# Two of four k chunks turned by DMA in fp16 parts, and the order of every engine laid out anew, in a batched attention and feed-forward kernel

## The reference

```
q = softmax(Wq LN(x), over the 64 rows of each of 8 heads) / 8      # 512 x 1024
k = softmax(Wk ctx, over the 1024 columns); v = Wv ctx              # 512 x 1024
a = Wo (per head: (v k^T) q) + bo
x = x + a / max(|a| of each column, 1e-12) * g * sqrt(128)
x = x + (LN(x) @ W4 + bias)     # W4: 1024 x 1024, 4-bit numbers with a scale and a zero for each output
```

## Time and profile before

| | us |
|---|---|
| median of 3 runs | 670.4 |
| lowest and highest | 669.9, 672.28 |
| the profiled execution, its own time | 670.46 |
| its span in the trace | 668.7 |
| PE busy, share of the span | 633.6, 95% |
| DVE busy | 550.3, 82% |
| POOL busy | 468.5, 70% |
| ACT busy | 455.1, 68% |

### The profile page before, as it was taken

One profiled execution on the slowest core, in us unless ns is written; L12 is line 12 of the kernel. 1 busy time (PEld: TensorE's weight loads), 2 busy tenths in 40 slices (PEclk: granted clock), 3 DMA queues, 4 the chain that ended last, 5 costly groups with the idle time before them and its releaser, 6 DMA issues.

```text
span 668.7 us, 10173 instructions
## 1 busy us (share of the span) xinstructions
PE 633.6 (95%) x3285; PEld 385.1 (58%) x3302; DVE 550.3 (82%) x897; ACT 455.1 (68%) x741; POOL 468.5 (70%) x409
## 2 busy tenths in 40 slices
PE   3869699999999999999999999999999999999987
PEld 2536365565656656565665656656665656566443
DVE  5786898888888888798888889888888988888854
ACT  3566868577775858777585867768586876858532
POOL 4166575977869596886959687795959778695930
PEclk9959899999999999999999999999999999999999
DMA  8153424756354565735355574635547453524551
GB/s 304 43 121 79 93 57 94 190 96 153 84 132 116 93 181 96 189 63 154 84 96 172 96 190 72 157 80 108 153 95 190 94 144 87 117 65 94 111 143 63
DMA packets 179236, 79.35 MB, mean 119 GB/s; under 512 B 168536, under 2 KB 170096, under 8 KB 179184
## 3 DMA queue, kind: packets, MB, share of 16 engines
q1 hardware_dynamic: 172848, 55.64, 40.2%
q10 hardware_dynamic: 6336, 23.07, 10.2%
HBM read 28.85 MB, written 8.39 MB: 56 GB/s over the span
## 4 chain that ended last, share of the span: by engine, by line
PE 83%; DVE 6%; ACT 3%; POOL 3%; issue 2%; DMA 1%; another core or an unknown queue 0%; SPq 0%; POOLq 0%; DVEq 0%; ACTq 0%
PE ps_m L1224 14%; PE ps_m L1319 14%; PE ps_k L1154 5%; PE ps_ta L1208 4%; PE ps_k L1155 4%; PE ps_k L1156 4%; PE ps_q L1154 4%; PE ps_q L1156 4%; PE ps_q L1155 4%; PE ps_tb L1208 4%; PE ps_o L1156 4%; PE ps_o L1154 4%; PE ps_o L1155 4%; PE ps_o L1419 4%; PE ps_o L1237 2%
## 5 line engine op out<-in xcount | busy, mean ns | idle before, releaser
L457 POOL TENSOR_TENSOR q_tok_lo<-q_exp,q_tok_hi 128x1024 f16<-128x1024 f32 x64 | 137.7, 2153 | 90.0 <-ACT q_tok_hi L611 88.4
L430 POOL TENSOR_TENSOR q_exp<-q_exp,q_rec 128x1024 f32<-128x1024 f32 x64 | 121.7, 1902 | 5.0
L586 ACT ACTIVATE k_exp<-ps_k,k_nmax 128x1024 f32<-128x1024 f32 x64 | 71.0, 1109 | 76.7 <-DVE k_nmax L858 76.7
L1224 PE MATMUL ps_m<-k_t,c_t 128*128 128x512 f32 x256 | 119.1, 599 | 0.0
L600 ACT ACTIVATE q_exp<-q_exp,w_unit 128x512 f32<-128x512 f32 x128 | 92.0, 720 | 39.0 <-DVE q_exp L870 39.0
L865 DVE TENSOR_REDUCE q_nmax<-ps_q 128x8 f32<-128x512 f32 x128 | 87.7, 685 | 27.6 <-PE ps_q L1156 27.2
L858 DVE TENSOR_REDUCE k_nmax<-ps_k 128x1 f32<-128x1024 f32 x64 | 77.3, 1208 | 19.7 <-PE ps_k L1156 19.7
L870 DVE TENSOR_TENSOR q_exp<-ps_q,q_nmax 128x512 f32<-128x512 f32 x128 | 88.5, 692 | 4.4
L611 ACT ACTIVATE q_tok_hi<-q_exp 128x1024 f16<-128x1024 f32 x64 | 67.5, 1055 | 23.6 <-POOL q_exp L430 23.6
L877 DVE TENSOR_REDUCE q_sum<-q_exp 128x16 f32<-128x1024 f32 x64 | 77.3, 1209 | 0.9 <-ACT q_exp L600 0.8
L1154 PE MATMUL ps_k<-c_hi,wk_lo 128*128 128x512 f32 x128 | 67.5, 527 | 3.3 <-ACT k_exp L586 3.2
(11 more groups left out here) (191 smaller groups left out, 1292.5 us busy)
## 6 DMA issues: line engine op xcount, KB each, us to landing
x_res<-in_x ACTq DMA_DIRECT2D x16, 512.0 KB, 3.8
out_x<-y SPq DMA_DIRECT2D x15, 512.0 KB, 2.9
x_in<-in_x ACTq DMA_DIRECT2D x14, 512.0 KB, 5.5
c_in<-in_ctx ACTq DMA_DIRECT2D x14, 512.0 KB, 6.2
x_in<-in_x SPq DMA_DIRECT2D x2, 512.0 KB, 5.8
c_in<-in_ctx SPq DMA_DIRECT2D x2, 512.0 KB, 7.7
q_hi<-q_tok_hi SPq DMA_TRANSPOSE x64, 3.1
q_lo<-q_tok_lo SPq DMA_TRANSPOSE x64, 3.2
```

The source lines that it names most:

```text
L430: nc.gpsimd.tensor_tensor(pair, pair, rec.unsqueeze(2).to_broadcast([P, 2 * HEADS, DH]), ALU.mult).then_inc(qs_done, 1)
L457: nc.gpsimd.tensor_tensor(q_tok_lo[p % 2][:], q_exp[:, 2 * p:2 * p + 2, :].rearrange("p t d -> p (t d)"), q_tok_hi[p % 2][:], ALU.subtract ...
L1224: last = nc.tensor.matmul(ps_m[:], c_t[s][:, t, :], k_t[:, t, :], start=(t == 0), stop=(t == TC - 1))
```

## The change

Chunks 0 and 1 of k are no longer turned on PE. Both are projected for the next batch at a period's end. Their exponentials are lifted by a factor 2^12 (`k_bias`), cut into an fp16 part on ACT (`high_k`) and the rest on POOL (`low_k`), and turned by four DMA transposes on SP's queue (`turn_k`). The turned context is scaled by `c_fit` and kept in f32, in fp16 and as an fp16 rest (`move_tc` has two operations for each half, `low_tc` is new on DVE, with `fit_c` and `undo_g` in place of `fit_g`). `mix_m` makes, for each t, three fp16 matmuls of 256 columns for chunks 0 and 1 and one f32 matmul of 256 columns for chunks 2 and 3. `split_rs` goes from ACT to POOL. `sum_q` of pair 3 goes from the end of its period to the next one, behind `low_x2`, and the order of all engines is laid out anew; `reciprocal` of k's sums goes to mid-period. In the set-up, splits and projections of the first batch come before the preparation of rows, which moves to period 0; the 4-bit weights are unpacked in other places, two at a time, with x2n_hi and x2n_lo lying in `spare`. The core of the diff (PE's, ACT's and DVE's order for periods after 0; indented less than in the file):

```diff
+k_lift = sb("k_lift", [P, 1])
+k_bias = sb("k_bias", [P, TURNED])
+k_hi = [sb(f"k_hi{j}", [P, N], F16) for j in range(TURNED)]
+k_lo = [sb(f"k_lo{j}", [P, N], F16) for j in range(TURNED)]
+k_t_hi = sb("k_t_hi", [P, TC, TURNED * P], F16)
+k_t_lo = sb("k_t_lo", [P, TC, TURNED * P], F16)
+k_t = sb("k_t", [P, TC, HID - TURNED * P])
...
+    def turn_k(b, j, name):
+        tok, turned, done, turned_sem = ((k_hi, k_t_hi, khi_done, khi_turned) if name == "hi" else
+                                         (k_lo, k_t_lo, klo_done, klo_turned))
+        sp.wait_ge(done, TURNED * b + j + 1)
+        if b > 0:
+            sp.wait_ge(m_ready, b)
+        sp.dma_start_transpose(turned[:, :, j * P:(j + 1) * P], tok[j][:]).then_inc(turned_sem, 16)
...
         if do_c:
             turn_q(c, 2, "hi")
+            turn_q(c, 2, "lo")
+        if do_a:
+            turn_k(a, 0, "hi")
...
         if do_f:
...
-            sp.dma_start_transpose(x2_hi[:], x2n_hi[:]).then_inc(x2hi_turned, 16)
+            sp.dma_start_transpose(x2_hi, x2n_hi).then_inc(x2hi_turned, 16)
+            sp.wait_ge(x2lo_done, f + 1)
+            sp.dma_start_transpose(x2_lo, x2n_lo).then_inc(x2lo_turned, 16)
+        if do_a:
+            turn_k(a, 0, "lo")
+            turn_k(a, 1, "hi")
         if do_c:
-            turn_q(c, 2, "lo")
             turn_q(c, 3, "hi")
-        if do_f:
-            sp.wait_ge(x2lo_done, f + 1)
-            sp.dma_start_transpose(x2_lo[:], x2n_lo[:]).then_inc(x2lo_turned, 16)
+        if do_a:
+            turn_k(a, 1, "lo")
         if do_c:
             turn_q(c, 3, "lo")
         if do_a:
...
+        def low_k(b, j):
+            pool.wait_ge(khi_done, TURNED * b + j + 1)
+            if begun(b):
+                pool.wait_ge(klo_turned, 16 * TURNED * b)
+            nc.gpsimd.tensor_tensor(k_lo[j][:], k_exp[:, j, :], k_hi[j][:], ALU.subtract).then_inc(klo_done, 1)
...
+        def split_rs():
+            pool.wait_ge(x2n_done, f + 1)
...
+        if do_f:
+            fit_x2(f)
+        low_k(a, 0)
+        if do_f:
+            split_rs()
+        if do_c:
+            scale_q(c, 3)
+        low_k(a, 1)
+        if do_c:
+            low_q(c, 3)
         if i == 0:
...
         def exp_k(b, sums, j):
             act.wait_ge(kmax_done, 4 * b + j + 1)
-            if begun(8 * b + 2 * (j - 2) + 2):
-                act.wait_ge(tk_ready, 8 * b + 2 * (j - 2) + 2)
-            nc.scalar.activation(k_exp[:, j % 2, :], ps_k[:], ACT.Exp, bias=k_nmax[:, j:j + 1],
+            bias = k_nmax[:, j:j + 1]
+            if j < TURNED:
+                if begun(b):
+                    act.wait_ge(kexp_done, 4 * (b - 1) + j + 1)
+                nc.scalar.activation(k_bias[:, j:j + 1], bias, ACT.Identity,
+                                     bias=k_lift[:]).then_inc(kbias_done, 1)
+                act.wait_ge(kbias_done, TURNED * b + j + 1)
+                bias = k_bias[:, j:j + 1]
+            held, of = (j - 2, b) if j >= 2 else (j + 2, b - 1)
+            if of >= 0:
+                if held < TURNED:
+                    act.wait_ge(klo_done, TURNED * of + held + 1)
+                else:
+                    act.wait_ge(tk_ready, TK * of + 2 * (held - TURNED) + 2)
+            nc.scalar.activation(k_exp[:, j % 2, :], ps_k[:], ACT.Exp, bias=bias,
                                  accum_out=k_sum[:, sums, j:j + 1]).then_inc(kexp_done, 1)
 
-        first = i == FIRST
+        def high_k(b, j):
+            act.wait_ge(kexp_done, 4 * b + j + 1)
+            if begun(b):
+                act.wait_ge(khi_turned, 16 * TURNED * b)
+                act.wait_ge(klo_done, TURNED * (b - 1) + j + 1)
+            nc.scalar.activation(k_hi[j][:], k_exp[:, j, :], ACT.Copy).then_inc(khi_done, 1)
...
         def move_tc(h):
 
+            turned = (ps_ta, ps_tb)[h][:].rearrange("p (t c) -> p t c", t=4)
             act.wait_ge(tc_ready, 2 * n + h + 1)
+            act.wait_ge(cfit_steps, 2 * (n + 1))
             if h == 0 and begun(n - 1):
                 act.wait_ge(m_ready, n - 1)
-            nc.scalar.activation(c_t[1 - s][:, 4 * h:4 * h + 4, :],
-                                 (ps_ta, ps_tb)[h][:].rearrange("p (t c) -> p t c", t=4),
-                                 ACT.Copy).then_inc(tc_moved, 1)
+            nc.scalar.activation(c_t_hi[1 - s][:, 4 * h:4 * h + 4, :], turned, ACT.Identity,
+                                 scale=c_fit[:]).then_inc(cthi_done, 1)
+            nc.scalar.activation(c_t[1 - s][:, 4 * h:4 * h + 4, :], turned, ACT.Identity,
+                                 scale=c_fit[:]).then_inc(tc_moved, 1)
...
+        else:
+            move_m()
+            if do_f:
                 normalise_x2()
...
+            exp_q(0)
+            if do_f:
                 high_x2()
...
+            exp_k(a, s, 2)
+            high_k(a, 1)
+            if do_n:
+                high_c()
+            exp_q(1)
+            high_q(c, 3)
+            move_tk(0)
+            move_tk(1)
+            if do_f:
+                move_rs()
...
+            exp_q(2)
+            exp_k(a, s, 3)
+            squares(0)
+            exp_q(3)
+            high_q(a, 0)
+        move_tk(2)
+        move_tk(3)
+        exp_q(4)
...
+        exp_q(5)
+        if do_c:
+            squares(1)
+        load_ahead()
+        high_q(a, 1)
+        exp_q(6)
+        if do_n:
+            move_tc(0)
+            high_x()
+            exp_k(n, 1 - s, 0)
+            high_k(n, 0)
+        exp_q(7)
+        if do_n:
+            move_tc(1)
+        high_q(a, 2)
+        if do_n:
+            exp_k(n, 1 - s, 1)
...
+        def fit_c():
+            dve.wait_ge(ctop_done, n + 1)
+            if begun(n):
+                dve.wait_ge(fit_steps, 2 * n)
+                dve.wait_ge(ctlo_done, 2 * n)
+                dve.wait_ge(tc_moved, 2 * n)
+            nc.vector.tensor_scalar(c_unit[:], c_top[:], UNIT_FLOOR, 1.0 / C_RANGE, ALU.max,
+                                    ALU.mult).then_inc(cfit_steps, 1)
+            dve.wait_ge(cfit_steps, 2 * n + 1)
+            nc.vector.reciprocal(c_fit[:], c_unit[:]).then_inc(cfit_steps, 1)
+        def low_tc(b, sb_, h):
+            dve.wait_ge(tc_moved, 2 * b + h + 1)
+            nc.vector.scalar_tensor_tensor(out=c_t_lo[sb_][:, 4 * h:4 * h + 4, :].rearrange("p t c -> p (t c)"),
+                                           in0=(ps_ta, ps_tb)[h][:], scalar=c_fit[:],
+                                           in1=c_t_hi[sb_][:, 4 * h:4 * h + 4, :].rearrange("p t c -> p (t c)"),
+                                           op0=ALU.mult, op1=ALU.subtract).then_inc(ctlo_done, 1)
...
+            shift_q(0)
+            split_g(c)
+            max_k(a, 2)
+            low_tc(a, s, 1)
+            if do_f:
                 low_x2(f)
-            if j == 3 and do_f:
+            sum_q(c, 3)
+            shift_q(1)
+            max_k(a, 3)
...
+            shift_q(2)
+            sum_q(a, 0)
+            shift_q(3)
+            if do_f:
...
                 scale_y(0)
...
+        if do_n:
+            abs_c()
...
+        shift_q(4)
+        invert_k()
...
+        sum_q(a, 1)
+        if do_f and i != END:
+            scale_y(1)
+        shift_q(5)
+        if do_n:
+            stats_x()
+            mean_x()
+        shift_q(6)
+        undo_g()
+        if do_c:
+            floor_n2()
...
+        top_c()
+        fit_c()
+        norm_x()
+        max_k(n, 0)
+        sum_q(a, 2)
+        low_tc(n, 1 - s, 0)
+        shift_q(7)
+        if do_c:
+            for h in range(HALVES):
+                attend(c, h)
+        max_k(n, 1)
+        if do_c:
+            stats_x2(x2)
...
-                last = nc.tensor.matmul(ps_m[:], c_t[s][:, t, :], k_t[:, t, :], start=(t == 0),
+                three(ps_m[:, 0:TURNED * P], c_t_hi[s][:, t, :], c_t_lo[s][:, t, :], k_t_hi[:, t, :],
+                      k_t_lo[:, t, :], start=(t == 0), stop=False)
+                last = nc.tensor.matmul(ps_m[:, TURNED * P:], c_t[s][:, t, :], k_t[:, t, :], start=False,
                                         stop=(t == TC - 1))
...
+        project_q(0)
...
+        else:
+            mix_g()
+            project_k(a, 2)
+            project_q(1)
+            mix_out(0)
+            project_k(a, 3)
+            transpose_k(0)
+            transpose_k(1)
+            project_q(2)
+        if do_f:
+            spread_rs()
+            feed_forward(0, (0,))
+        project_q(3)
+        if do_f:
+            feed_forward(0, (1,))
+        transpose_k(2)
+        project_q(4)
+        transpose_k(3)
...
+        if do_f and i != END:
+            feed_forward(1, (0, 1))
+        project_q(5)
+        if do_c:
+            mix_out(1)
+        project_q(6)
+        if do_n:
+            transpose_c(0)
+        if do_c:
+            norm_rows()
+        if do_n:
+            spread_c()
+            project_k(n, 0)
+        if i == END:
+            project_q(7)
+        mix_m(0, 4)
+        if do_n:
+            project_q(7)
+        if do_c:
```

(30 more changed lines are left out.)

664 lines of the change are left out of this document (313 added, 351 removed).

## The result

The changed kernel takes 664.0 us (median of 4, 660.96 to 665.57), the kernel before 670.6 (669.9 to 672.28) in the same session: ratio 0.9897, 95% interval 0.9872 to 0.9921. The forecast of 656 us had -14.6; the profiled executions give 663.18 - 670.46 = -7.3. The sign and the range (643 to 669) hold, the size is half of the forecast.

The account below looks back on a forecast made before the run. It took PE as the old bound and a chain round POOL as the new one, 37.9 us a period; terms of -7.8, -3.2, -2.6, -1.0 and 0 make -14.6 from 670.46: 656 us, range 643 to 669.

Parts of the forecast that it names:

- The steady part: 12 steady periods, each falling from 38.55 to 37.9 us: -7.8 us in all, bounds -31 to +4.
- 32.1 + 5.7 = 37.85: Round of the POOL chain: 32.1 us POOL work without a gap, 5.7 through normalise_x2, high_x2, low_x2 and sum_q.
- the 37.7 of PE's chain: Second chain, through PE, per period: 36.0 us of work plus 1.4 and 0.3 of waits.
- low_x2 at 1.23: DVE's low_x2 falls into POOL's only gap and takes its shortest time, 1.23 us; 2.22 kept for the range.
- period 0, "-1.0; bounds +2 and -3": Period 0: DVE gets the preparation of rows, k's exponentials follow each other with fewer turns between; -1.0 us.
- Periods 1 and 2: Periods with about 1 us of unpacking each: from 39.6 to 38.0 us each, -3.2 in all, bounds 0 and -6.
- The start: Set-up: splits go first, so the first q0 comes near 15.8 instead of 18.42 us; -2.6, bounds 0 and -3.5.
- The drain: Period 15 and drain: everything after POOL's last scale_q and low_q as before; 0 us, bounds +1 and -2.
- The POOL chain: Rival: low_x2 or norm_x waits for a POOL operation, 0.7 us a period, 666 us or 669; chance 0.22.
- no load came out from under a pass: Rival: weight loads of mix_m's narrow passes are not hidden; 683 us for half, some 710 for all; chance 0.10.
- PE was not the bound: Rival: PE stays the bound, DVE and POOL overlap better, period 36.0 to 37.0, 630 to 643 us; chance 0.12.
- Late transposes: Rival: 14 DMA transposes on one queue make PE wait; 680 us if all 3.2 is lost, 656 to 668 if half; chance 0.08.

Follow-up runs that it names:

- the product behind low_c: Changed kernel plus an unused POOL product of 128x256 elements behind low_c in periods 3 to 14; 670.5 us in one run, period 38.40.
- the fastest version: Changed kernel, q's last sum in its own period, set_up_rows and bogs_col early, period 1's picks later, batch 1's picks ending period 0; 649.2 us.
- the version without the later sum: Changed kernel with sum_q of q's last pair back at the end of its own period; 654.9 us, ratio 0.9765 to the kernel before.
- the start alone: Changed kernel with the fastest version's new order of periods 0 and 1, q's last pair still summed in the next period; 659.9 us.
- set_up_rows early: Changed kernel with set_up_rows before max_k(1) in period 0, nibble picks of batches 0 and 1 behind max_k(2) and sum_q(0); 663.5 us.

## Why the prediction was half right

- **The steady part: right.** The bound, the order of the terms, and the sum (32.1 + 5.7 = 37.85) were measured as 31.94 + 5.74 = 37.68, and the product behind low_c shows that the chain binds. "I take 37.9" added a loss between two chains that isn't there. PE's own sum was too low (36.0; the busy time in the fastest version is 439.4 us over 12 periods, 36.6) and its waits too high (1.7; PE stood 0.94); the 37.7 of PE's chain met the period by two errors that cancel. The forecast did not ask what the chain costs: the version without the later sum shows that it costs 0.7 us a period against PE's bound.
- **low_x2 at 1.23: right, and the reason too.** The Trainium skill, "SBUF — State Buffer", section "Who interferes with whom", has the later of the two wait out the whole of the other. The runs agree: 3.21 behind low_k, 1.81 behind a product of 0.74, 1.23 without one, and POOL's 2.76 instead of 1.90 where DVE came first. They go further at one place: bogs_col waited out two POOL instructions.
- **The step that failed: period 0, "-1.0; bounds +2 and -3".** It measured +5.5, outside its bounds, and the term has no row behind it. Its text says "DVE gets that preparation", and I weighed the exponentials' spacing and not DVE's queue: the preparation stood ahead of max_k(2), in a stage where POOL had newly got low_k. With only the order of DVE and of ACT's conversions changed (the start alone) the stage measured 39.8 us (15.52 to 55.30) instead of 44.3, +0.9 against the kernel before and inside the bounds. I had priced low_x2 by the instruction beside it and did so for no other DVE instruction, though in these runs the products of set_up_rows (2.21 instead of 0.28) and the picks (3.05 instead of 0.69) are held in the same way. Where the 1.9 us come from that this still is above the forecast's 37.9 stays open; executions with the same instructions differ by more in this stage.
- **Periods 1 and 2: -3.2 forecast, -0.5 measured.** The picks in front of shift_q(2) took 2.60 and 2.50 us instead of 0.68; the kernel before had its own picks held too (1.83 and 2.17), but not two in a row. Moving them won 0.6 us of that period. But they aren't the cause by themselves: with the sum in its own period they stand at the same place and take 0.68 and 0.69, and period 1 is 42.20. In the experiments period 1 takes 40 to 44 us, and PE's waits for q_exp in it come to 4.2 us or more; the fastest version still has a pick of 2.21 between shift_q(3) and shift_q(4) there. What bounds this period was not tried and stays open.
- **The start: right.** -3.1 against -2.6, though other executions have it between 14.1 and 17.0 us instead of 15.3.
- **The drain: +1.3, above its bound of +1, and not by the change.** Two experiments with the same instructions in it have 35.4 us (set_up_rows early) and 38.1 (the start alone). In the changed kernel PE's granted clock is 0.62 from 638 to 642 us, and 1.00 in the same stretch of the run with 35.4. That the clock is the whole of it was not tested.
- **Rivals.** The POOL chain did not slip, no load came out from under a pass, PE waited for a DMA only once behind the set-up, 0.34 us in the drain, and PE was not the bound. The slower side had no part. Late transposes show only where the POOL chain is gone, as said above.

## What to carry over

When a change gives POOL new work, list every DVE instruction with two SBUF inputs (and the picks, tensor_scalar from SBUF to SBUF) that can now meet it, in the start as well as in the steady part, and ask of each whether PE waits behind it: in these runs its price was the rest of POOL's instruction, whatever its own size, and in two runs the whole of POOL's next one too. Idle time of one engine can be what keeps another at its speed; before filling a gap, see who runs in it, and if need be put a wait in front of the filler. A new chain through several engines is worth pricing piece by piece, for one moved instruction (here a sum of 1.5 us) may cost more than half of what the rest won (9 of 16 us).
